# Dropping the matmuls with unread results from most of a pipeline's drain

## The reference

```python
x = x + _L0_conv_ref(_gn(x), ...)      # windowed attention: shift by 4, 8x8 windows, 16 heads of 32, relative positions, masks
t = _to_tokens(x)                      # 16 images of 256 tokens
t = t + _L1_attn_ref(_ln_t(t), ...)    # attention of an image's 256 tokens, 8 heads of 16
t = t + _L1_ffn_ref(_ln_t(t), ...)     # 8 experts, the best 2 of each token, silu(h1) * h2, weighted sum
```

## Time and profile before

| | before |
|---|---|
| median of 3 runs | 706.4 us |
| the profiled execution, its own time | 709.77 us |
| its span (first to last instruction) | 708.0 us |
| granted TensorE clock, mean over the span | 0.954 |
| busy: TensorE matmuls / VectorE / ScalarE / GpSimd | 598.8 / 438.5 / 410.4 / 396.2 us |
| iterations 15 and 16, about | 437 to 487 us |
| iterations 17 to 19, about | 487 to 527 us |
| last scatter of the pipeline, start | 546.5 us |

### The profile page before, as it was taken

One profiled execution on the slowest core, in us unless ns is written; L12 is line 12 of the kernel. 1 busy time (PEld: TensorE's weight loads), 2 busy tenths in 40 slices (PEclk: granted clock), 3 DMA queues, 4 the chain that ended last, 5 costly groups with the idle time before them and its releaser, 6 DMA issues.

```text
span 708.0 us, 18292 instructions
## 1 busy us (share of the span) xinstructions
PE 598.8 (85%) x6460; PEld 479.6 (68%) x6460; DVE 438.5 (62%) x1325; ACT 410.4 (58%) x915; POOL 396.2 (56%) x503
## 2 busy tenths in 40 slices
PE   4877889999989899899899998988975799999910
PEld 3656667777767777677677776766655688888810
DVE  5534666767767677677776777765433365555625
ACT  2445576787676667766767677444411366666600
POOL 5665653454546576665665765642376066666643
PEclk9799999999999999999999999999996899999975
DMA  7100220231422414224133242243841122233237
GB/s 213 25 2 1 54 54 13 50 69 56 120 43 91 118 37 119 57 86 126 42 104 89 66 122 57 85 124 91 270 182 49 47 87 87 84 91 91 72 135 254
DMA packets 54511, 63.08 MB, mean 89 GB/s; under 512 B 12978, under 2 KB 47794, under 8 KB 53906
## 3 DMA queue, kind: packets, MB, share of 16 engines
q1 hardware_dynamic: 48294, 49.59, 25.3%
q0 software_dynamic: 4544, 9.38, 3.9%
q10 hardware_dynamic: 1584, 2.95, 1.2%
HBM read 35.74 MB, written 28.64 MB: 91 GB/s over the span
## 4 chain that ended last, share of the span: by engine, by line
PE 42%; POOL 17%; issue 15%; DVE 10%; ACT 7%; DMA 6%; SPq 2%; ACTq 0%; DVEq 0%; POOLq 0%
POOL slots L549 5%; POOL pa L623 4%; POOL pa L631 3%; PE pG L1192 3%; PE pSA L1264 3%; DMA slots<-sel_dram 2%; PE pSB L1438 2%; PE pTA L1438 2%; PE pTB L1438 2%; PE pSA L1438 2%; PE pTA L1349 2%; DVE pa L994 2%; PE pOA L1449 2%; PE pOB L1449 2%; PE pOB L1293 2%
## 5 line engine op out<-in xcount | busy, mean ns | idle before, releaser
L623 POOL TENSOR_TENSOR pa<-pa,mxa 128x512 f32<-128x512 f32 x64 | 66.7, 1042 | 110.9 <-DVE mxa L1017 110.8
L664 POOL DMA_INDIRECT ysl<-yo,dst x78 | 75.5, 968 | 59.7 <-DVE yo L1154 45.3
L631 POOL TENSOR_TENSOR pa<-pa,rca 128x512 f32<-128x512 f32 x64 | 67.0, 1047 | 63.5 <-DVE rca L1037 63.3
L760 ACT ACTIVATE ptb<-pTB 128x512 f32<-128x512 f32 x128 | 76.6, 599 | 43.1 <-PE pTB L1275 42.7
L549 POOL DMA_INDIRECT slots<-rec,slot x64 | 65.1, 1017 | 15.9 <-issue 13.2
L777 ACT ACTIVATE pta<-pTA 128x512 f32<-128x512 f32 x64 | 38.5, 602 | 56.1 <-PE pTA L1349 55.6
L1027 DVE TENSOR_REDUCE sma<-pa 128x8 f32<-128x512 f32 x64 | 43.8, 684 | 37.8 <-ACT pa L754 37.8
L754 ACT ACTIVATE pa<-pa 128x512 f32<-128x512 f32 x64 | 40.2, 628 | 42.2 <-POOL pa L623 41.9
L1349 PE MATMUL pTA<-ident,pa 128*128 128x128 f32 x256 | 40.3, 281 | 24.0 <-DVE pa L994 14.7
L979 DVE TENSOR_REDUCE mxb<-pSA 128x2 f32<-128x512 f32 x64 | 44.0, 688 | 25.1 <-PE pSA L1240 24.5
L1275 PE MATMUL pTB<-q,kbd 100*128 100x256 f32 x256 | 56.1, 301 | 0.1
(11 more groups left out here) (227 smaller groups left out, 1738.3 us busy)
## 6 DMA issues: line engine op xcount, KB each, us to landing
slots<-sel_dram SPq DMA_DIRECT2D x16, 1040.0 KB
kbd<-kst SPq DMA_DIRECT2D x128, 48.0 KB, 2.2
q<-qst SPq DMA_DIRECT2D x64, 96.0 KB, 2.2
xt<-slots SPq DMA_DIRECT2D x39, 130.0 KB, 2.2
xch<-x_ch_dram SPq DMA_DIRECT2D x4, 512.0 KB, 5.8
xt<-x_tok_dram SPq DMA_DIRECT2D x16, 128.0 KB, 2.3
xch<-t SPq DMA_DIRECT2D x16, 128.0 KB, 4.6
fw<-f_dram SPq DMA_DIRECT2D x1, 2048.0 KB
```

The lines of the kernel that those rows point to most:

```text
L623: pool.tensor_tensor(pa[:, u, :, :], pa[:, u, :, :], mxa[:, u % 2, :].unsqueeze(2).to_broadcast([128, 8, WIN]), ALU.subtract).then_inc(sa_ ...
L631: pool.tensor_tensor(pa[:, u, :, :], pa[:, u, :, :], rca[:, b, :].unsqueeze(2).to_broadcast([128, 8, WIN]), ALU.mult).then_inc(sa_nrm, 1)
L664: pool.indirect_dma_start(ysl, bass.IndirectOffsetOnAxis(ap=dst[:, t % YB, n:n + 1], axis=0), yo[:, t % YB, n, :], None).then_inc(y_dma[t ...
L760: a.activation(ptb[:, h % PTBUFS, :, :], pTB[:, :].rearrange("p (a b) -> p a b", a=2), ACT.Exp).then_inc(st_exp, 1)
```

## The change

The three conditions for keep_awake into pG become one. Before, two calls stood in each step of iterations 15 (but for n = 0) and 16, four in each of 17 and 18, four in n = 3 and 5 of 19. Now there are two in each step of iteration 18, where image 15 is T, and two in n = 3 and 5 of iteration 19. The wait for g_ev, which stood before those of iterations 15 and 16, stands before these.

```diff
                 for n in range(8):
                     if A is not None and M is not None and Bm is None:
                         keep_awake(pSB, 1)
-                    if G is None and Bm is not None and M is not None:
-                        if n > 0 or A is None:
-                            pe.wait_ge(g_ev, B * GU)
-                            keep_awake(pG, 2)
-                    elif A is None and R is not None and (T is not None or n in (3, 5)):
-                        keep_awake(pG, 4)
+                    if Bm is None and R is not None and (T is not None or n in (3, 5)):
+                        pe.wait_ge(g_ev, B * GU)
+                        keep_awake(pG, 2)
                     if Bm is not None:
```

## The result

The change makes the kernel slower, by less than 1%. The new kernel takes 713.56 us (median of 9 runs, 711.92 to 718.52), the old one beside it 711.17 (9 runs, 704.63 to 718.87); the ratio of the runs is **1.008, 95% interval 1.0049 to 1.0111**, which is 3.5 to 7.9 us more. I had forecast 706.0 against 706.4, so no change.

The account below looks back on a forecast made before the run. Other engines and image 13's exchange write, not TensorE's fillers (keep_awake matmuls nobody reads), were taken to bound most of the drain. 0 + 0 + 0 + 0.9 - 0.5 = 0.4 us less: 706.0 against 706.4, range 703.0 to 709.3.

Parts of the forecast that it names:

- The clock, 0.5 us, bounds 0 and 1.7: Iterations 15 and 16: TensorE's busy share sinks without fillers, so clock falls may come; 0.5 us lost, between 0 and 1.7.
- The 1.1 us in hand: Iteration 16, root of image 15's variance: VectorE's input was ready at 475.47, GpSimd took it at 476.55; TensorE has 1.1 us spare.
- Rival C: Iterations 15 to 17: the kernel gets slower by the clock, about 18.4 us of real TensorE pieces exposed; chance 0.20.
- Iterations 15 and 16, gain 0: Removing their 14 and 16 fillers gains 0, as other waits cover them; upper bounds 3.2 and 3.7 us.
- Iteration 17, gain 0: Image 14's t2 waits for the previous t2's write to xch, so it stays at 511.64; at most 0.7 us gained.
- the 5.2 us that TensorE was to gain: Iteration 17 and n=0, 1 of 18: fillers worth 8.4 us less 3.2 covered; TensorE 5.2 us earlier at image 14's output projection.
- Iteration 18, gain 0.9: Rest of iteration 18: GpSimd's 0.97 us wait for the root at 524.80 is all the end can inherit; gain 0.9.
- The pause of 4.4 us: Before iteration 18's four-head group: TensorE, ready at about 507.7, would stand until 512.1, 4.4 us where it stood 0.3.
- A: No DMA holds t2, so iteration 17's 5.2 us come too: 6.1 us less, 700.3; chance 0.12.
- B: The chain taken at its word across the drain: 15.2 us less, 691.2; chance 0.03.
- D: Nothing of the drain's end depends on these fillers; the 0.9 is lost too, no fall: 706.4, no change; chance 0.03.
- The range of the forecast: Whole kernel: the forecast's own range is 703.0 to 709.3 us; for 8 in 10 it is 702.5 to 712.5.

Follow-up runs that it names:

- the earlier write: The first expert's weight loads issued after iteration 17 instead of 16, all 102 fillers kept, against the old kernel: 707.70 us, ratio 0.9999.

## Why the prediction was wrong

- **The clock, 0.5 us, bounds 0 and 1.7: the step that failed.** In the two traces of the change the way from the drain's start to t2 of image 13 is 5.2 and 5.3 us longer (3.35 + 1.82 - 0.01; 3.34 + 1.99), three times my upper bound. I had put it on the rows myself (busy 0.66 without the fillers, against a stretch of 0.79 that held and one of 0.54 that ended in a fall), and then paid for half of one stay of 3.4 us at most and took the rest as slack. That stay, behind a pause of TensorE in 51 to 55 us, is in the trace of before (0.90, 0.50, 0.50, 0.50 and 0.90 over the five us from 55 to 60, with L1337 at 3.56 us against 1.95); that one more of this length, half of it lost, would be the most, and the 0.5 us itself, were my guess; no run shows them. The removal in 15 and that in 16 bring a fall each, and each keeps TensorE at half clock for about 10 us, not 3.4; in after it is 13.6 us over 450 to 480 (0.83, 0.85, 0.64) and 17 more over 490 to 510. A fall is worth 2.9 and 2.7 us in the traces. Why so much reaches the end: at half clock the projections and scores for which ScalarE, VectorE and GpSimd wait are themselves up to twice as long (a projection 2.92 or 3.62 us against 1.95, a score matmul 0.80 against 0.40), and each engine's slack had been measured with TensorE at full speed. The 1.1 us in hand at GpSimd's root in 476.55 was gone: VectorE had its input ready at 480.25 (L986, 480.08 + 0.17) instead of 475.47, just when GpSimd ended its scatters, at 480.26. And GpSimd was itself 3.7 us late, because its row there starts with the root behind t2 of image 12 (L601, 476.81 instead of 473.07), which hangs on TensorE's matmuls (L1413) and not only on the copy of the maxima that I had let hide the fillers.
- **Rival C, chance 0.20, is what came:** slower by the clock, 3.5 to 7.9 us in the first comparison and 3.9 in the drain. My estimate for it was 5.8 us more: half of its 18.4 us of real pieces at half clock (0.50), 9.2 us, less 2.5 for slack and 0.9 for iteration 18. On 706.4 that is 712.2; that it also lies near the measured 713.56 is partly chance, since before stood at 711.17 beside it. Its mechanism, its place (15 to 17) and its effect on SyncE's queue are in the rows; its price was a guess at half clock over half of 439 to 487, and the clock was mostly above that in this stretch (0.83, 0.85, 0.64 and 1.00 by tens from 450 us) and lower behind it (0.55, 0.60). My objection, that TensorE fills up at half clock and the clock comes back, is true (1.00 over 480 to 490) and no objection: it comes back after the matmuls on the path have paid (L1334, L1413). In after no long wait stood ahead of the fall at 467 us (0.53 over 467 to 468, 0.50 over the nine us behind it): TensorE's longest from 455 us on was 0.86 us.
- **Iterations 15 and 16, gain 0.** The three intervals up to t2 of image 13 became no more than 0.1 us shorter in any kernel with these fillers out; but none of those ran at full clock throughout, so whether they would give anything at 1.00 stays open. One reading under it was wrong: GpSimd does not work without a pause from the bookkeeping matmuls of iteration 15 on. It stands 1.96 us behind them (they end at 444.06), for VectorE, whose step comes behind t2 of image 11; TensorE sets that time, and without the fillers of 15 the wait is 3.73. Before, then without those of 15:

```profile
446.26 1.04 POOL L623 TENSOR_TENSOR pa<-pa,mxa 128x512 f32<-128x512 f32 x1 [1.96 <-DVE mxa L1017]
```
```profile
452.35 1.04 POOL L623 TENSOR_TENSOR pa<-pa,mxa 128x512 f32<-128x512 f32 x1 [3.73 <-DVE mxa L1017]
```

- **Iteration 17, gain 0.** The size was right (0.29 less in "13 to 14", with 0.77 us of waiting for the write), the reading half wrong. The write is next, 0.33 us behind, but TensorE held t2 in before, not the write. And of the 5.2 us that TensorE was to gain, little existed in after: at clock 0.55 and 0.60 its projection of image 14 comes 15.98 us after t2 of image 13 (514.41 - 498.43), against 16.74 in before.
- **Iteration 18, gain 0.9.** Confirmed: 10.70 us between the roots, no idle time, and 1.34 us less from t2 to t2, in after and in the run with this part alone.
- **The pause of 4.4 us** of TensorE before the four-head group of iteration 18 did not come in after, nor a fall at 512 (1.00 over 510 to 530): the clock had fallen earlier and TensorE had nothing to wait with. With fillers in 15 to 17 to hold the clock and half of them gone from 17 on, a pause of 1.71 us and a fall did come there.
- **Rivals A and B.** A's first half (no DMA holds t2 in before) is true, its gain is not: the write stands 0.33 us behind. And with the write out of the way the kernel without fillers in 17 was no faster than before (1.0017). Nothing in the traces speaks for B. D is out, since the 0.9 us came.
- **The range of the forecast.** Its upper end does not follow from its own terms: 706.4 + 1.7 + 2 is 710.1, not 709.3. The measured 713.56 lies outside both.

## What to carry to other kernels

Slack on an engine's neighbours that was read at full clock is not slack any more if the edit can slow that engine down; price a fall on every real matmul of the stretch whose results another engine waits for, not on the stay alone (here one fall, 10.2 us at half clock, cost 2.9 us and another 2.7). Where unread matmuls hold the clock, as two a step did here over 490 to 510 us (1.00, against 0.50 and 0.50 or 0.82 without them), halve them before dropping them, stage by stage, and look at the clock of each stage. And where two bounds stand close behind each other, lift both: here half of the fillers gave 0.1% (not clear of nothing) and the earlier write nothing, each alone, and 0.5 to 0.6% together.

## What was not expected

- Two fillers a step held the clock at 1.00 over 490 to 510 in all three traces that have them, and none let it fall to 0.50 over 490 to 500 in both that lack only those of 17 among 15 to 17: the same engine, the same real work.
- With all fillers of 15 in place the clock still fell in three of the eight traces that keep them and those of 16 (0.78 to 0.94 by tens, over ten to thirty us between 430 and 480): in the kernel without those of 17, and in two of those with later loads. It may be part of what scatters the runs of before, 704.6 to 718.9 us. The tie is weak: of the 34 runs of before with a clock on record, the slower half has a mean of 0.953, the faster half 0.957.
- Fillers behind a fall did not make it cheaper: the kernel without those of 15 and 16 has 4 a step behind them, and its "12 to 13" is longer than that of the whole change (24.86 against 23.62). Why is open; one trace of each is too little. Its drain as a whole (114.69 us against 112.29) is also longer because it lacks the 1.34 us of iteration 18.
